# The last 64 channels' low-part product in two 64-row halves of the array, in the tail of a vision-tower kernel

## The chip, the cores and the metric

The kernel runs on one core of one Trainium2 chip. The time is the device time of one execution in microseconds, the median of three runs. A profile of one execution stands beside it: its span goes from the first to the last instruction, and its own device time is given with it.

## The reference

Two images of 32 channels and 128 x 128 pixels become 256 tokens each. A token mixer (patch embedding to 128 channels, two transformer layers) is followed by a head to 192 channels. The tail works at that width, and is the part that the change touches:

```
h   = _ln(x, lnf_g, lnf_b) @ head_w + head_b          # 256 tokens x 192 channels
# linear attention, 12 heads of 16, _phi(x) = elu(x) + 1
qkv = _layernorm(h) @ W_qkv                           # 192 -> 3 x 192
...                                                   # k^T v, q (k^T v) / z
h   = h + attention @ W_out + b_out
# feed-forward, weights multiplied by a mask that is mixed from alpha_e, alpha_r
h   = h + gelu(_layernorm(h) @ w_fc + b_fc) @ w_proj + b_proj     # 192 -> 768 -> 192
```

(The tail's lines are abridged here into one form; the products and their sizes are the reference's.)

## The kernel before

The program is written out by hand, one instruction list per engine, with counting semaphores between them. Nothing but the order of the lines sets the order of the work. The two images go through the same steps, and one image's products are placed where the other waits for VectorE (DVE) or ScalarE (ACT).

TensorE (PE) multiplies 32-bit numbers in two ways here. Plain products (`head`, `attend3`, `numerators3`, `proj3`, the transposes) take their operands as they are. Products that need accuracy at the fast rate are split: each operand is the sum of a high part and a low part, both of type fp32r, and the product is high x high + high x low + low x high. In the tail two products are split: `rows192` (query and key together 384 columns wide as `qk3_high`/`qk3_low`, the value 192 wide as `v3_rows`) and `fc3` (six chunks of 128 hidden units by 256 tokens).

The 192 channels don't fit the 128 rows of the array. Channels 0 to 127 are one contraction of 128 rows: three products, high x high, high x low, low x high. The last 64 channels are stacked: rows 0 to 63 of `yT3_rest` hold the input's high part, rows 64 to 127 its low part, and the host has put the weight's rows 128 to 191 in both halves. One product with the weight's high part (`aqkvw_parts[0][:, 1, :]`, `fcw_parts[0][:, 1, :]`) gives high x high + low x high. One more with the weight's low part gives high x low; for it the rows 64 to 127 of the weight's low part are set to zero, so half of the array multiplies zeros. That is five products for each output: L454, L455, L457, L458, L459 in `rows192`, L503 to L507 in `fc3`.

The input parts are made after a transpose (`turn3`, L339 and L340) into PSUM: DVE writes the high part (`high_part3`, L1046), ACT copies the last 64 channels' high part (`evict`, L1558), DVE writes their low part into rows 64 to 127 (`rest_low_part3`) and then the low part of the first 128 (`low_part3`, both L969). ACT turns the qk product into the elu feature (L1593, L1597), scales the value (L1601) and computes the gelu (L1607). `fc3`'s chunks lie two to a PSUM bank, and so do the value's two token tiles.

Two 64-row products side by side are in the kernel already, in `value_out` (L390): its odd and even products take rows 0 to 63 and 64 to 127, and write two banks.

Of the kernel before, what the change touches and what calls it, by code (L numbers as in the profile page):

```python
# [12 lines left out]
P = 128  # L13
# [11 lines left out]
E = 192  # L25
# [32 lines left out]
def build(nc, small, convb, norm_rows0, norm_rows1, ff_norm_rows0, ff_norm_rows1, embed0, patches1, qkv_w, rest_w, rows, mix, fc_w, proj_w,  # L58
          head_w, aqkv_w, aout_w, out):
    with ExitStack() as ctx:  # L60
# [64 lines left out]
        def bias_row(name, n=0, width=D):  # L125
# [17 lines left out]
        yT3_hi, yT3_lo, yT3_rest = (per_image(f"yT3_{part}", [P, TOKENS], F32R) for part in ("hi", "lo", "rest"))  # L143
# [59 lines left out]
        TURN4_BANK = [bank[3], bank[5]]  # L203
        TURN4_REST_BANK = [bank[4], bank[1]]
        V3_BANK = [bank[3], bank[0]]
# [6 lines left out]
        PROJ3_BANK = [(bank[0], bank[3]), (bank[4], bank[5])]  # L212
        FC3_BANK = [(bank[3], bank[2], bank[6]), (bank[5], bank[0], bank[0])]
# [42 lines left out]
            sem(n) for n in ("y_ready", "y_turned",))  # L256
        consts_set = sem("consts_set")
# [54 lines left out]
        def _(pe):  # L312
# [136 lines left out]
            def rows192(dst, i, t, at, stages):  # L449


                tile = slice(t * P, (t + 1) * P)
                if "high" in stages:
                    nc.tensor.matmul(dst, yT3_hi[i][:, tile], aqkvw_parts[0][:, 0, at], start=True, stop=False)  # L454
                    mm = nc.tensor.matmul(dst, yT3_hi[i][:, tile], aqkvw_parts[1][:, 0, at], start=False, stop=False)  # L455
                if "low" in stages:
                    nc.tensor.matmul(dst, yT3_lo[i][:, tile], aqkvw_parts[0][:, 0, at], start=False, stop=False)  # L457
                    nc.tensor.matmul(dst, yT3_rest[i][:, tile], aqkvw_parts[0][:, 1, at], start=False, stop=False)  # L458
                    mm = nc.tensor.matmul(dst, yT3_rest[i][:, tile], aqkvw_parts[1][:, 1, at], start=False, stop=True)  # L459
                return mm  # L460

            def qk3_high(i, t):
                return rows192(QK3_BANK[i][t][:, 0:2 * E], i, t, slice(0, 2 * E), ("high",))

            def qk3_low(i, t):
                return rows192(QK3_BANK[i][t][:, 0:2 * E], i, t, slice(0, 2 * E), ("low",))

            def v3_rows(i, t):
                return rows192(V3_BANK[i][:, t * E:(t + 1) * E], i, t, slice(2 * E, 3 * E), ("high", "low"))

# [15 lines left out]
            def numerators3(i):  # L486
                for t in range(TILES):
                    for c in range(ECH):
                        at = (t * ECH + c) * KVW
                        mm = nc.tensor.matmul(NUM3_BANK[i][:, at:at + KVW], qT3[i][:, c, t * P:(t + 1) * P],  # L490
                                              kv3[i][:, c, :], start=True, stop=True)
                return mm

            def attend3(i, t):
                for c in range(ECH):
                    mm = nc.tensor.matmul(ATT3_BANK[i][:, t * E:(t + 1) * E], attT3[i][:, c, t * P:(t + 1) * P],  # L496
                                          aoutw[:, c, :], start=(c == 0), stop=(c == ECH - 1))
                return mm

            def fc3(i, c):  # L500
                at = slice(c * P, (c + 1) * P)
                dst = FC3_BANK[i][c // 2][:, (c % 2) * TOKENS:(c % 2 + 1) * TOKENS]
                nc.tensor.matmul(dst, fcw_parts[0][:, 0, at], yT3_hi[i][:], start=True, stop=False)  # L503
                nc.tensor.matmul(dst, fcw_parts[1][:, 0, at], yT3_hi[i][:], start=False, stop=False)
                nc.tensor.matmul(dst, fcw_parts[0][:, 0, at], yT3_lo[i][:], start=False, stop=False)
                nc.tensor.matmul(dst, fcw_parts[0][:, 1, at], yT3_rest[i][:], start=False, stop=False)
                return nc.tensor.matmul(dst, fcw_parts[1][:, 1, at], yT3_rest[i][:], start=False, stop=True)  # L507
# [46 lines left out]
            pe.wait_ge(consts_set, 14)  # L554
# [275 lines left out]
            qk3_high(0, 0)  # L830
            qk3_high(0, 1)
# [8 lines left out]
            v3_rows(0, 0).then_inc(v3_done, 1)  # L840
            v3_rows(0, 1).then_inc(v3_done, 1)
# [21 lines left out]
            v3_rows(1, 0).then_inc(v3_done, 1)  # L863
            v3_rows(1, 1).then_inc(v3_done, 1)
# [14 lines left out]
            fc3(0, 2).then_inc(fc3_done, 1)  # L879
            pe.wait_ge(gelu3_ready, 1)  # L880
            proj3(0, 0, 0).then_inc(proj3_done, 1)
            pe.wait_ge(attention3_columns, 2)
            attend3(1, 0).then_inc(out3_done, 1)
            attend3(1, 1).then_inc(out3_done, 1)
            pe.wait_ge(gelu3_ready, 2)
            proj3(0, 0, 1).then_inc(proj3_done, 1)
            fc3(0, 3).then_inc(fc3_done, 1)
            proj3(0, 1, 0).then_inc(proj3_done, 1)
            proj3(0, 1, 1).then_inc(proj3_done, 1)
            pe.wait_ge(gelu3_ready, 3)  # L890
# [4 lines left out]
            fc3(0, 4).then_inc(fc3_done, 1)  # L895
            fc3(0, 5).then_inc(fc3_done, 1)
# [8 lines left out]
            proj3(0, 5, 1).then_inc(proj3_done, 1)  # L905
            pe.wait_ge(low4, 2)
            fc3(1, 0).then_inc(fc3_done, 1)
            fc3(1, 1).then_inc(fc3_done, 1)
            pe.wait_ge(out_ready, 1)
            fc3(1, 2).then_inc(fc3_done, 1)  # L910
            fc3(1, 3).then_inc(fc3_done, 1)
            pe.wait_ge(gelu3_ready, 7)
            proj3(1, 0, 0).then_inc(proj3_done, 1)
            pe.wait_ge(gelu3_ready, 8)
            proj3(1, 0, 1).then_inc(proj3_done, 1)
            proj3(1, 1, 0).then_inc(proj3_done, 1)
            proj3(1, 1, 1).then_inc(proj3_done, 1)
            pe.wait_ge(gelu3_ready, 9)
# [3 lines left out]
            fc3(1, 4).then_inc(fc3_done, 1)  # L922
            fc3(1, 5).then_inc(fc3_done, 1)
# [10 lines left out]
        def _(dve):  # L934
# [116 lines left out]
            def rest_low_part3(i, bankof):  # L1051
                return low_part(yT3_rest[i][EB:P, :], bankof[0:EB, 0:TOKENS], yT3_rest[i][0:EB, :])
# [56 lines left out]
            dve.wait_ge(consts_set, 14)  # L1109
# [336 lines left out]
            rest_low_part3(0, TURN3_REST_BANK[0])  # L1446
# [32 lines left out]
            dve.wait_ge(rest_high3, 2)  # L1479
            rest_low_part3(1, TURN3_REST_BANK[1])  # L1480
# [33 lines left out]
            rest_low_part3(0, TURN4_REST_BANK[0])  # L1514
# [25 lines left out]
            dve.wait_ge(rest_high4, 2)  # L1540
            rest_low_part3(1, TURN4_REST_BANK[1])
# [14 lines left out]
        def _(act):  # L1556
# [43 lines left out]
            def v3_to_sbuf(i, t):  # L1600
                return nc.scalar.activation(v3[i][:, t, :, 0:EC],  # L1601
                                            V3_BANK[i][:, t * E:(t + 1) * E].rearrange("p (n e) -> p n e", e=EC),
                                            ACT.Copy, scale=rstd[i][:, t:t + 1])

            def gelu3(i, c):
                src = FC3_BANK[i][c // 2][:, (c % 2) * TOKENS:(c % 2 + 1) * TOKENS]
                return nc.scalar.activation(hid3[i][:, c, :], src, ACT.Gelu_apprx_tanh, bias=fcb[:, c:c + 1])  # L1607
# [157 lines left out]
            evict(yT3_rest[0][0:EB, :], TURN3_REST_BANK[0][0:EB, 0:TOKENS]).then_inc(rest_high3, 1)  # L1765
            act.wait_ge(qk3_done, 1)
# [14 lines left out]
            evict(yT3_rest[1][0:EB, :], TURN3_REST_BANK[1][0:EB, 0:TOKENS]).then_inc(rest_high3, 1)  # L1781
            act.wait_ge(qk3_done, 3)
# [14 lines left out]
            evict(yT3_rest[0][0:EB, :], TURN4_REST_BANK[0][0:EB, 0:TOKENS]).then_inc(rest_high4, 1)  # L1797
            act.wait_ge(fc3_done, 2)
# [11 lines left out]
            evict(yT3_rest[1][0:EB, :], TURN4_REST_BANK[1][0:EB, 0:TOKENS]).then_inc(rest_high4, 1)  # L1810
            act.wait_ge(fc3_done, 8)
# [10 lines left out]
        def _(pool):  # L1822
# [41 lines left out]
            pool.wait_ge(consts_set, 14)  # L1864
# [3 lines left out]
            low_part(aqkvw_parts[1][0:EB, 1, :], aqkvw[0:EB, 1, :], aqkvw_parts[0][0:EB, 1, :])  # L1868
# [63 lines left out]
            low_part(fcw_parts[1][0:EB, 1, :], fcw[0:EB, 1, :], fcw_parts[0][0:EB, 1, :])  # L1932
# [81 lines left out]
```

## Time and profile before

| what | us |
|---|---|
| median of 3 runs | 129.16 (128.75 to 129.81) |
| profiled execution, device time | 129.22 |
| its span | 126.8 |
| PE busy | 117.3 (93%) |
| DVE busy | 77.0 (61%) |
| ACT busy | 62.9 (50%) |
| GpSimd (POOL) busy | 45.9 (36%) |

The device time is 2.4 us more than the span; that is the launch and the end, which the span leaves out. The tail begins near 87.5 us. Records of PE overlap: a matmul's record has its whole way through the array in it, so what one product costs a busy PE is the distance from its start to the next start, not its length.

### The profile page before, as it was taken

The page shows a single profiled execution, that of the slowest core. Times are in us where ns is not written, and L with a number is a line of the kernel's source. Part 1 is how long each engine was busy: PE and PEld are TensorE (multiplying, and loading weights), DVE is VectorE, ACT ScalarE, POOL GpSimd, SP SyncE. Part 2 cuts the span into 40 slices and gives each one's busy share as a digit, 9 for nine tenths or more (in the row PEclk, how much of TensorE's full clock was granted, in tenths as well). Part 3 has the DMA queues.
Part 4 walks back from the last instruction along what each step waited for, and adds up shares of the span by engine and source line. Part 5 has one row for each costly group of instructions (what it writes and reads, how often), then busy time and mean ns, then how long its engine had stood idle before and what let it go on. Part 6 is the DMA issues. An engine that isn't in the chain of part 4 may idle for free.

```text
span 126.8 us, 2258 instructions
## 1 busy us (share of the span) xinstructions
PE 117.3 (93%) x852; PEld 101.2 (80%) x852; DVE 77.0 (61%) x244; ACT 62.9 (50%) x151; POOL 45.9 (36%) x56
## 2 busy tenths in 40 slices
PE   6999979999999999999999899977989988999991
PEld 6989968985978778997856689966777877998990
DVE  5000264996787766679999897639498377155002
ACT  4000142844579478194774876534871735423520
POOL 0000024034599833204939858475214032031000
PEclk9999999999999999999999999999999999999999
DMA  4999799999600000000000000000000000000101
GB/s 106 353 418 433 228 435 393 386 421 414 185 0 0 0 3 5 0 0 0 0 0 5 0 0 0 3 5 0 0 0 0 0 0 5 0 0 0 62 0 62
DMA packets 4171, 12.43 MB, mean 98 GB/s; under 512 B 473, under 2 KB 2105, under 8 KB 3906
## 3 DMA queue, kind: packets, MB, share of 16 engines
q1 hardware_dynamic: 4162, 12.31, 26.0%
q8 instruction: 6, 0.10, 0.3%
q14 instruction: 3, 0.02, 0.1%
HBM read 11.91 MB, written 0.39 MB: 97 GB/s over the span
## 4 chain that ended last, share of the span: by engine, by line
PE 65%; DVE 12%; DMA 9%; ACT 4%; issue 3%; SPq 3%; POOL 2%; DVEq 0%; ACTq 0%; POOLq 0%
DMA norm_rows_sb<-in_norm_rows 9%; PE bank L405 6%; PE bank L510 6%; PE bank L424 5%; PE bank L381 4%; PE bank L325 4%; PE bank L398 3%; PE bank L376 3%; SPq L265 3%; PE bank L346 3%; PE bank L412 2%; PE bank L358 2%; PE bank L496 2%; PE bank L334 2%; PE bank L390 2%
## 5 line engine op out<-in xcount | busy, mean ns | idle before, releaser
L1824 POOL TENSOR_TENSOR rstd<-mv,minus_half 128x2 f32<-128x2 f32 x14 | 10.0, 716 | 47.8 <-DVE mv L942 47.8
L1842 POOL TENSOR_TENSOR qn<-q,rqsum 128x512 f32<-128x512 f32 x8 | 8.3, 1042 | 10.5 <-DVE rqsum L1012 10.5
L1607 ACT ACTIVATE patches_sb<-bank,fcb 128x256 f32<-128x256 f32 x12 | 5.1, 469 | 10.5 <-PE bank L507 10.5
L1565 ACT ACTIVATE kexp<-bank,nkmax 128x256 f32<-128x256 f32 x16 | 7.5, 472 | 5.7 <-DVE nkmax L992 5.7
L405 PEld LDWEIGHTS bank<-cw,qT 128*128 128x128 f32 x64 | 8.0, 191 | 2.4 <-issue 1.5
L405 PE MATMUL bank<-cw,qT 128*128 128x128 f32 x64 | 8.9, 280 | 0.7 <-DVE x L1027 0.4
L510 PE MATMUL bank<-projw,patches_sb 128*128 128x192 f32 x48 | 9.4, 331 | 0.0
L325 PE MATMUL bank<-embed_sb 128*128 128x128 f32 x64 | 8.7, 291 | 0.3 <-DMA embed_sb<-in_embed 0.3
L424 PE MATMUL bank<-restw,hid 128*128 128x128 f32 x64 | 8.8, 281 | 0.1
L325 PEld LDWEIGHTS bank<-embed_sb 128*128 128x128 f32 x64 | 8.0, 200 | 1.1 <-DMA embed_sb<-in_embed 1.1
L1558 ACT ACTIVATE x<-bank 128x128 f32<-128x128 f32 x4 | 1.1, 282 | 14.4 <-DVE stats L936 14.4
L1581 ACT ACTIVATE hid<-bank,small_sb 128x256 f32<-128x256 f32 x16 | 6.5, 472 | 3.6 <-PE bank L419 3.6
L424 PEld LDWEIGHTS bank<-restw,hid 128*128 128x128 f32 x64 | 7.8, 191 | 0.6 <-issue 0.3
L936 DVE BATCH_NORM_STATS2 stats<-bank 128x6 f32<-128x128 f32 x4 | 1.1, 274 | 11.7 <-PE bank L330 11.6
L510 PEld LDWEIGHTS bank<-projw,patches_sb 128*128 128x128 f32 x48 | 7.6, 189 | 0.5 <-ACT patches_sb L1607 0.4
L381 PE MATMUL bank<-ktok,y 128*128 128x512 f32 x16 | 8.0, 612 | 0.0
L325 PE MATMUL bank<-embed_sb,patches_sb 128*128 128x128 f32 x64 | 7.9, 277 | 0.0
L325 PEld LDWEIGHTS bank<-embed_sb,patches_sb 128*128 128x128 f32 x64 | 7.5, 192 | 0.2 <-DMA patches_sb<-in_patches 0.2
L992 DVE TENSOR_REDUCE nkmax<-bank 128x2 f32<-128x512 f32 x8 | 5.4, 688 | 3.0 <-PE bank L365 2.9
L1834 POOL TENSOR_TENSOR xb<-x,rows_sb 128x256 f32<-128x256 f32 x8 | 5.8, 730 | 3.6 <-DVE xn L978 2.4
L969 DVE TENSOR_TENSOR yT_lo<-bank,yT_hi 128x256 fp32r<-128x256 f32 x12 | 5.1, 422 | 2.9 <-ACT yT_hi L1558 2.8
L1577 ACT ACTIVATE cw<-bank,rksum 128x128 f32<-128x128 f32 x16 | 4.8, 364 | 3.8 <-PE bank L398 3.8
(165 smaller groups left out, 333.0 us busy)
## 6 DMA issues: line engine op xcount, KB each, us to landing
embed_sb<-in_embed SPq DMA_DIRECT2D x3, 768.0 KB, 7.7
patches_sb<-in_patches SPq DMA_DIRECT2D x2, 1024.0 KB, 12.5
restw<-in_rest_w SPq DMA_DIRECT2D x2, 768.0 KB, 15.6
qkvw<-in_qkv_w SPq DMA_DIRECT2D x3, 256.0 KB, 11.7
qkvw<-in_qkv_w SPq DMA_DIRECT2D x1, 768.0 KB, 15.7
fcw<-in_fc_w SPq DMA_DIRECT2D x1, 768.0 KB, 18.3
embed_sb<-in_embed SPq DMA_DIRECT2D x1, 576.0 KB, 4.4
aqkvw<-in_aqkv_w SPq DMA_DIRECT2D x1, 576.0 KB, 12.2
```

Source lines behind the costliest of these rows:

```text
L325: mm = nc.tensor.matmul(CONV_BANK[i][t][:, 0:D], left, embed_sb[:, c, 0:D], start=(c == 0), stop=False)
L381: return nc.tensor.matmul(YK_BANK[s][:], y[s % IMAGES][:, t, :], ktok[:, t, :], start=(t == 0), stop=(t == TILES - 1))
L405: mm = nc.tensor.matmul(ATT_BANK[s][t][:, 0:D], qT[:, t, c * P:(c + 1) * P], cw[:, c, :], start=(c == 0), stop=(c == PAIRS - 1))
L424: mm = nc.tensor.matmul(FF2_BANK[s][t][:, 0:D], hid[:, c, t * P:(t + 1) * P], ff2w(s // IMAGES, c), start=(c == 0), stop=(c == FC - 1))
L510: return nc.tensor.matmul(PROJ3_BANK[i][t][:, 0:E], hid3[i][:, c, t * P:(t + 1) * P], projw[:, c, :], start=(c == 0), stop=(c == HC - 1))
L969: return nc.vector.tensor_tensor(lo, exact, hi.bitcast(F32), ALU.subtract)
L992: return nc.vector.tensor_reduce(nkmax[i][:, 2 * b:2 * b + 2], K_BANK[s][b][:].rearrange("p (c t) -> p c t", c=2), AX_X, ALU.max, negate=True)
L1565: return nc.scalar.activation(kexp[:, c, :], K_BANK[s][c // 2][:, (c % 2) * TOKENS:(c % 2 + 1) * TOKENS], ACT.Exp, bias=nkmax[i][:, c:c + ...
L1581: return nc.scalar.activation(hid[:, c, :], FF1_BANK[s][c // 2][:, (c % 2) * TOKENS:(c % 2 + 1) * TOKENS], ACT.Gelu, bias=col("ff1_b", s / ...
L1824: return nc.gpsimd.tensor_tensor(rstd[i][:], mv[i][:, :, 1], minus_half[:], ALU.pow)
L1834: return nc.gpsimd.tensor_tensor(xb[i][:], x[i][:], row.unsqueeze(1).to_broadcast([P, TILES, D]), ALU.add)
L1842: return nc.gpsimd.tensor_tensor(qn[:, t, :].rearrange("p (h d) -> p h d", h=HEADS), q[:, t, :].rearrange("p (h d) -> p h d", h=HEADS), rq ...
```

## The change

The zero half of the array is given work. The weight's low part now holds its 64 rows twice (no zeros). Two outputs are worked on together: after the high products and the products with the weight's high part, the low-part product of the first output runs in rows 0 to 63 and that of the second in rows 64 to 127. The second needs the input's high part in rows 64 to 127 as well, so ACT makes a copy, `rest3_copy`, four times. Each of the two outputs needs its own PSUM bank; `FC3_BANK`, `V3_BANK`, `PROJ3_BANK` and the transposes' banks are dealt out anew. The products with `yT3_lo` come last. In the feed-forward PE starts on the high part (`high4`) instead of waiting for `low4`, the chunks come in pairs, and projections are moved behind them. DVE loses two memsets at the start; POOL subtracts all 128 rows where it did 64.

```diff
-        V3_BANK = [bank[3], bank[0]]
+        V3_BANK = [(bank[3], bank[0]), (bank[0], bank[5])]
-        PROJ3_BANK = [(bank[0], bank[3]), (bank[4], bank[5])]
-        FC3_BANK = [(bank[3], bank[2], bank[6]), (bank[5], bank[0], bank[0])]
+        PROJ3_BANK = [(bank[0], bank[4]), (bank[1], bank[7])]
+        FC3_BANK = [bank[3], bank[2], bank[6], bank[5], bank[3], bank[2]]
...
+            def rows192_rest(bank_of, i, at, n):
+                for t in range(TILES):
+                    nc.tensor.matmul(bank_of[t][:, 0:n], yT3_rest[i][:, t * P:(t + 1) * P], aqkvw_parts[0][:, 1, at],
+                                     start=False, stop=False)
+                for t in range(TILES):
+                    rows, left = slice(t * EB, (t + 1) * EB), (yT3_rest, rest3_copy)[t]
+                    mm = nc.tensor.matmul(bank_of[t][:, 0:n], left[i][rows, t * P:(t + 1) * P],
+                                          aqkvw_parts[1][rows, 1, at], start=False, stop=False)
+                return mm
...
+            def fc3_rest(i, pair):
+                for c in (2 * pair, 2 * pair + 1):
+                    nc.tensor.matmul(FC3_BANK[c][:, 0:TOKENS], fcw_parts[0][:, 1, c * P:(c + 1) * P], yT3_rest[i][:],
+                                     start=False, stop=False)
+                for odd in range(2):
+                    rows, c, right = slice(odd * EB, (odd + 1) * EB), 2 * pair + odd, (yT3_rest, rest3_copy)[odd]
+                    mm = nc.tensor.matmul(FC3_BANK[c][:, 0:TOKENS], fcw_parts[1][rows, 1, c * P:(c + 1) * P],
+                                          right[i][rows, :], start=False, stop=False)
+                return mm
...
+            pe.wait_ge(high4, 1)
+            fc3_high(0, 0)
+            pe.wait_ge(rest_low4, 1)
+            pe.wait_ge(rest_high4, 2)
+            fc3_rest(0, 0)
             pe.wait_ge(low4, 1)
-            fc3(0, 0).then_inc(fc3_done, 1)
-            fc3(0, 1).then_inc(fc3_done, 1)
+            fc3_low(0, 0).then_inc(fc3_done, 1)
+            fc3_low(0, 1).then_inc(fc3_done, 1)
...
-            nc.vector.memset(aqkvw_parts[1][EB:P, 1, :].bitcast(F32), 0.0).then_inc(consts_set, 1)
-            nc.vector.memset(fcw_parts[1][EB:P, 1, :].bitcast(F32), 0.0).then_inc(consts_set, 1)
...
             evict(yT3_rest[0][0:EB, :], TURN3_REST_BANK[0][0:EB, 0:TOKENS]).then_inc(rest_high3, 1)
+            act.wait_ge(rest_high3, 1)
+            evict(rest3_copy[0][EB:P, :], yT3_rest[0][0:EB, :].bitcast(F32)).then_inc(rest_high3, 1)
...
-            low_part(fcw_parts[1][0:EB, 1, :], fcw[0:EB, 1, :], fcw_parts[0][0:EB, 1, :])
+            low_part(fcw_parts[1][:, 1, :], fcw[:, 1, :], fcw_parts[0][:, 1, :])
```

The qk product of image 0 on PE (token tile 0 in bank 5, tile 1 in bank 1), from the first high product on; before:

```order
L454 MATMUL bank5<-aqkvw_hi,yT3_hi0 128x384 [waits high3]
L455 MATMUL bank5<-aqkvw_lo,yT3_hi0 128x384
L454 MATMUL bank1<-aqkvw_hi,yT3_hi0 128x384
L455 MATMUL bank1<-aqkvw_lo,yT3_hi0 128x384
L457 MATMUL bank5<-aqkvw_hi,yT3_lo0 128x384 [waits low3]
L458 MATMUL bank5<-aqkvw_hi,yT3_rest0 128x384
L459 MATMUL bank5<-aqkvw_lo,yT3_rest0 128x384
```

and with the change:

```order
L455 MATMUL bank5<-aqkvw_hi,yT3_hi0 128x384 [waits high3]
L455 MATMUL bank5<-aqkvw_lo,yT3_hi0 128x384
L455 MATMUL bank1<-aqkvw_hi,yT3_hi0 128x384
L455 MATMUL bank1<-aqkvw_lo,yT3_hi0 128x384
L463 MATMUL bank5<-aqkvw_hi,yT3_rest0 128x384 [waits rest_high3,rest_low3]
L463 MATMUL bank1<-aqkvw_hi,yT3_rest0 128x384
L467 MATMUL bank5<-aqkvw_lo,yT3_rest0 128x384
L467 MATMUL bank1<-aqkvw_lo,rest3_copy0 128x384
L472 MATMUL bank5<-aqkvw_hi,yT3_lo0 128x384 [waits low3]
```

Tile 0 used to be finished after seven products; it is now finished after nine, the two L467 being the 64-row pair. For image 1 it was finished after five (high, high, low, rest, rest), and is now finished after nine too.

The first two hidden chunks of the feed-forward of image 0 on PE; before:

```order
L503 MATMUL bank3<-yT3_hi0,fcw_hi 128x256 [waits low4]
L504 MATMUL bank3<-yT3_hi0,fcw_lo 128x256
L505 MATMUL bank3<-yT3_lo0,fcw_hi 128x256
L506 MATMUL bank3<-yT3_rest0,fcw_hi 128x256
L507 MATMUL bank3<-yT3_rest0,fcw_lo 128x256
L503 MATMUL bank3<-yT3_hi0,fcw_hi 128x256
```

and with the change:

```order
L524 MATMUL bank3<-yT3_hi0,fcw_hi 128x256 [waits high4]
L524 MATMUL bank3<-yT3_hi0,fcw_lo 128x256
L524 MATMUL bank2<-yT3_hi0,fcw_hi 128x256
L524 MATMUL bank2<-yT3_hi0,fcw_lo 128x256
L531 MATMUL bank3<-yT3_rest0,fcw_hi 128x256 [waits rest_high4,rest_low4]
L531 MATMUL bank2<-yT3_rest0,fcw_hi 128x256
L535 MATMUL bank3<-yT3_rest0,fcw_lo 128x256
L535 MATMUL bank2<-rest3_copy0,fcw_lo 128x256
L540 MATMUL bank3<-yT3_lo0,fcw_hi 128x256 [waits low4]
L540 MATMUL bank2<-yT3_lo0,fcw_hi 128x256
```

The number of products is the same, ten for two chunks; two of them (L535) are now 64 rows each, and stand between products of all 128 rows.

ACT at the start of the tail, with the change; the second row is new:

```order
L1613 ACTIVATE yT3_rest0<-bank7 64x256 [waits turned3]
L1613 ACTIVATE rest3_copy0<-yT3_rest0 64x256 [waits rest_high3]
L1648 ACT_TABLE_LOAD [waits deviation3_ready]
L1648 ACTIVATE embed_sb<-bank5,rstd0 128x384 [waits qk3_done]
```

The copy stands ahead of the load of the exp table and of the first elu instruction.

## Rows read from the trace of the kernel before

**Rows 1.** The page: busy times of the engines.

```profile
PE 117.3 (93%) x852; PEld 101.2 (80%) x852; DVE 77.0 (61%) x244; ACT 62.9 (50%) x151; POOL 45.9 (36%) x56
```

**Rows 2.** Busy time by stretch, the feed-forward: stretch, its length, each engine, granted clock (1.00 is full).

```profile
106.30:123.90 17.60, 17.57 (x124) 16.70 (x124) 4.98 (x17) 6.18 (x15) 1.71 (x2) 1.00 0.04 11
```

**Rows 3.** PE's timeline around `value_out`: start us, us, instruction, rows*columns of the array.

```profile
33.95 0.28 PE L358 MATMUL bank<-yT_hi,qkw_lo 128*128 128x256 f32 x1
34.06 0.28 PE L365 MATMUL bank<-yT_lo,qkw_hi 128*128 128x256 f32 x1
34.27 1.16 PE L390 MATMUL bank<-restw,qkvw 64*128 64x128 f32 x16
35.36 0.50 PE L346 MATMUL bank<-qkw_hi,yT_hi 128*128 128x512 f32 x1
35.70 0.39 PE L346 MATMUL bank<-qkw_lo,yT_hi 128*128 128x512 f32 x1
35.93 0.40 PE L352 MATMUL bank<-qkw_hi,yT_lo 128*128 128x512 f32 x1
```

**Rows 4.** Line 390 by itself: duration ns min/median/max, first and last start.

```profile
L390 PE MATMUL bank<-restw,qkvw x32: 271/272/374, 34.3 to 52.6; 64*128 64x128 f32 x32
```

**Rows 5.** PE's timeline, the attention of image 0, then of image 1.

```profile
88.69 0.44 PE L454 MATMUL bank<-aqkvw_hi,yT_hi 128*128 128x384 f32 x1 [0.52 <-DVE yT_hi L1046]
88.97 0.34 PE L455 MATMUL bank<-aqkvw_lo,yT_hi 128*128 128x384 f32 x1
...
89.32 0.33 PE L455 MATMUL bank<-aqkvw_lo,yT_hi 128*128 128x384 f32 x1
89.58 0.44 PE L457 MATMUL bank<-aqkvw_hi,yT_lo 128*128 128x384 f32 x1
...
90.04 0.34 PE L459 MATMUL bank<-aqkvw_lo,yT_rest 128*128 128x384 f32 x1
...
93.15 0.27 PE L459 MATMUL bank<-aqkvw_lo,yT_rest 128*128 128x192 f32 x1
...
94.24 0.94 PE L474 MATMUL bank<-v,embed_sb 128*96 128x102 f32 x8
...
96.62 0.42 PE L454 MATMUL bank<-aqkvw_hi,yT_hi 128*128 128x384 f32 x1
...
97.66 0.34 PE L459 MATMUL bank<-aqkvw_lo,yT_rest 128*128 128x384 f32 x1
```

**Rows 6.** The chain of waits: start us, us, what.

```profile
90.41 0.58 ACT embed_sb L1593
...
98.04 0.67 ACT embed_sb L1597
```

**Rows 7.** ACT's timeline: the last 64 channels' copy, the table, the value.

```profile
88.21 0.38 ACT L1558 ACTIVATE yT_rest<-bank 64x256 fp32r<-64x256 f32 x1 [1.74 <-PE bank L340]
88.61 1.28 ACT L1593 ACT_TABLE_LOAD   x1
...
93.46 0.73 ACT L1601 ACTIVATE v<-bank,rstd 128x192 f32<-128x192 f32 x2 [0.50 <-PE bank L459]
```

**Rows 8.** PE's timeline: the start of each image's feed-forward, and what is ahead of it.

```profile
104.72 1.08 PE L490 MATMUL bank<-kv,patches_sb 96*128 96x102 f32 x8
106.29 0.39 PE L503 MATMUL bank<-yT_hi,fcw_hi 128*128 128x256 f32 x1 [0.49 <-DVE yT_lo L969]
106.51 0.28 PE L504 MATMUL bank<-yT_hi,fcw_lo 128*128 128x256 f32 x1
...
114.85 1.53 PE L510 MATMUL bank<-projw,patches_sb 128*128 128x192 f32 x8
116.42 0.39 PE L503 MATMUL bank<-yT_hi,fcw_hi 128*128 128x256 f32 x1
```

**Rows 9.** DVE's timeline: the input parts of the feed-forward.

```profile
104.92 0.42 DVE L1046 CAST yT_hi<-bank 128x256 fp32r<-128x256 f32 x1 [0.32 <-PE bank L340]
...
105.81 0.42 DVE L969 TENSOR_TENSOR yT_lo<-bank,yT_hi 128x256 fp32r<-128x256 f32 x1
```

More of the change, by code:

```diff
@@ L142, in build @@
         yT_hi, yT_lo = (per_image(f"yT_{part}", [P, TOKENS], F32R) for part in ("hi", "lo"))
-        yT3_hi, yT3_lo, yT3_rest = (per_image(f"yT3_{part}", [P, TOKENS], F32R) for part in ("hi", "lo", "rest"))
+        yT3_hi, yT3_lo, yT3_rest, rest3_copy = (
+            per_image(name, [P, TOKENS], F32R) for name in ("yT3_hi", "yT3_lo", "yT3_rest", "rest3_copy"))
         nkmax = per_image("nkmax", [P, PAIRS])
@@ L447, in head @@
                                         start=True, stop=True)
[L449 to L459, printed above, removed]
-                return mm
@@ L462, in qk3_high, with rows192 @@
-            def qk3_high(i, t):
-                return rows192(QK3_BANK[i][t][:, 0:2 * E], i, t, slice(0, 2 * E), ("high",))
-            def qk3_low(i, t):
-                return rows192(QK3_BANK[i][t][:, 0:2 * E], i, t, slice(0, 2 * E), ("low",))
-            def v3_rows(i, t):
-                return rows192(V3_BANK[i][:, t * E:(t + 1) * E], i, t, slice(2 * E, 3 * E), ("high", "low"))
+            def rows192(bank_of, i, at, n):
+                for t in range(TILES):
+                    for part in range(2):
+                        mm = nc.tensor.matmul(bank_of[t][:, 0:n], yT3_hi[i][:, t * P:(t + 1) * P],
+                                              aqkvw_parts[part][:, 0, at], start=(part == 0), stop=False)
+                return mm
@@ new lines, in rows192_rest @@
+            def rows192_rest(bank_of, i, at, n):
+                for t in range(TILES):
+                    nc.tensor.matmul(bank_of[t][:, 0:n], yT3_rest[i][:, t * P:(t + 1) * P], aqkvw_parts[0][:, 1, at],
+                                     start=False, stop=False)
+                for t in range(TILES):
+                    rows, left = slice(t * EB, (t + 1) * EB), (yT3_rest, rest3_copy)[t]
+                    mm = nc.tensor.matmul(bank_of[t][:, 0:n], left[i][rows, t * P:(t + 1) * P],
+                                          aqkvw_parts[1][rows, 1, at], start=False, stop=False)
+                return mm
@@ new lines, in rows192_low, with qk3_high, qk3_rest @@
+            def rows192_low(bank_of, i, t, at, n):
+                return nc.tensor.matmul(bank_of[t][:, 0:n], yT3_lo[i][:, t * P:(t + 1) * P], aqkvw_parts[0][:, 0, at],
+                                        start=False, stop=True)
+            def qk3_high(i):
+                return rows192(QK3_BANK[i], i, slice(0, 2 * E), 2 * E)
+            def qk3_rest(i):
+                return rows192_rest(QK3_BANK[i], i, slice(0, 2 * E), 2 * E)
+            def qk3_low(i, t):
+                return rows192_low(QK3_BANK[i], i, t, slice(0, 2 * E), 2 * E)
@@ L471, in context3, with v3_high_and_rest, v3_low @@
+            def v3_high_and_rest(i):
+                at = slice(2 * E, 3 * E)
+                rows192(V3_BANK[i], i, at, E)
+                return rows192_rest(V3_BANK[i], i, at, E)
+            def v3_low(i, t):
+                return rows192_low(V3_BANK[i], i, t, slice(2 * E, 3 * E), E)
             def context3(i):
@@ L498, in attend3, with fc3_high, fc3_low @@
                 return mm
[L500 to L507, printed above, removed]
+            def fc3_high(i, pair):
+                for c in (2 * pair, 2 * pair + 1):
+                    for part in range(2):
+                        mm = nc.tensor.matmul(FC3_BANK[c][:, 0:TOKENS], fcw_parts[part][:, 0, c * P:(c + 1) * P],
+                                              yT3_hi[i][:], start=(part == 0), stop=False)
+                return mm
+            def fc3_rest(i, pair):
+                for c in (2 * pair, 2 * pair + 1):
+                    nc.tensor.matmul(FC3_BANK[c][:, 0:TOKENS], fcw_parts[0][:, 1, c * P:(c + 1) * P], yT3_rest[i][:],
[4 more added lines that the diff above has]
+                                          right[i][rows, :], start=False, stop=False)
+                return mm
+            def fc3_low(i, c):
+                return nc.tensor.matmul(FC3_BANK[c][:, 0:TOKENS], fcw_parts[0][:, 0, c * P:(c + 1) * P], yT3_lo[i][:],
+                                        start=False, stop=True)
             def proj3(i, c, t):
@@ L1781, in _ @@
             evict(yT3_rest[1][0:EB, :], TURN3_REST_BANK[1][0:EB, 0:TOKENS]).then_inc(rest_high3, 1)
+            act.wait_ge(rest_high3, 3)
+            evict(rest3_copy[1][EB:P, :], yT3_rest[1][0:EB, :].bitcast(F32)).then_inc(rest_high3, 1)
             act.wait_ge(qk3_done, 3)
@@ L1797, in _ @@
             evict(yT3_rest[0][0:EB, :], TURN4_REST_BANK[0][0:EB, 0:TOKENS]).then_inc(rest_high4, 1)
+            act.wait_ge(rest_high4, 1)
+            evict(rest3_copy[0][EB:P, :], yT3_rest[0][0:EB, :].bitcast(F32)).then_inc(rest_high4, 1)
             act.wait_ge(fc3_done, 2)
@@ L1810, in _ @@
             evict(yT3_rest[1][0:EB, :], TURN4_REST_BANK[1][0:EB, 0:TOKENS]).then_inc(rest_high4, 1)
+            act.wait_ge(rest_high4, 3)
+            evict(rest3_copy[1][EB:P, :], yT3_rest[1][0:EB, :].bitcast(F32)).then_inc(rest_high4, 1)
             act.wait_ge(fc3_done, 8)
```

94 lines of the change are left out of this document (56 added, 38 removed).

## The prediction

> **What bounds the kernel now.** I read the page first. PE is busy for 93% of the span [rows 1], so the question is what an edit costs PE. In the tail the busy times by stretch come next: from 106.3 us to 123.9 us, the two feed-forwards, PE is busy 17.57 of 17.60 us at full granted clock [rows 2]. There each 0.1 us more or less on PE moves the end by as much. Ahead of that, from 88 to 106 us, PE and ACT take turns. The chain of waits goes through ACT's first elu instruction of each image, L1593 at 90.41 and L1597 at 98.04 [rows 6], and both start when L459 ends, the product that finishes token tile 0: 90.04 + 0.34 = 90.38, and 97.66 + 0.34 = 98.00 [rows 5]. So two clocks count: when tile 0 of the query and key product is finished, and how long PE is occupied afterwards.
>
> The slot of one product is the distance between starts. At 256 columns it is 0.11 us (33.95 to 34.06) [rows 3]. At 384 columns I take 0.17 us, half of 89.32 less 88.97 [rows 5]. A first product after a stand costs more: 88.69 to 88.97 is 0.28 for 384 columns, 0.11 above the slot, because its weight load is not hidden.
>
> **What a lone 64-row pair costs.** The only 64-row pairs in the trace are those of `value_out` [rows 3, 4]. Their 16 records (each fp32 product is recorded twice) begin at 34.27, and the last begins at 34.27 + 1.16 - 0.27 = 35.16. The longest record is 374 ns, the median 272: the first ones carry an exposed weight load of 0.10. The rest is (0.89 - 0.10) / 7 = 0.11 us for each two records, so inside such a run two records do fit in one slot. The edges are another matter. Entry: 34.06 to 34.27 is 0.21 where the slot is 0.11, 0.10 lost. Exit: 35.16 to 35.36 is 0.20, 0.09 lost. The next 128-row product then takes 35.36 to 35.70 = 0.34 where the following takes 35.70 to 35.93 = 0.23: 0.11 more for its exposed load. Entry 0.10, load 0.10, exit 0.09, load 0.11: 0.40 us of edges. `value_out` has eight products to spread them over; the change makes a run of one pair, ten times, each between 128-row products. What it saves is one slot: 0.11 us at 256 or 192 columns, 0.17 at 384. So a pair costs PE 0.40 - 0.11 = **+0.29 us**, or +0.23 at 384 columns. No row shows fp32r operands in half the array, hence the bounds: with no edges -0.11 (-0.17), with edges and the two one behind the other +0.40. I take +0.29, since the run of line 390 is entered from fp32r products and left to them, as here.
>
> The Trainium skill ("TensorE: Matmul & The Clock Gate", Measured speedup vs the span model) has packed tiles take the time of one matmul and some 4 ns for each further tile; by that alone every pair would save its slot, and the sum below would be about -1.3 instead of +2.3. The trace agrees inside the run, not at its edges. The same skill ("TensorEngine Tiling (Array Packing)", Key Properties) says that a change of tiling mode drains the engine, and gives no time for it; the entry and exit gaps are what this trace shows of it.
>
> **Part by part.**
>
> - *Tile 0 of query and key, image 0.* High products start at 88.69, 88.97, 89.15, 89.32 as now [rows 5]. Then the two with the weight's high part, 89.49 and 89.66; the pair at 89.66 + 0.17 + 0.10 = 89.93; load 0.10, its columns 0.17, exit 0.09: the low product at 90.29, and with the exposed load it takes 0.44 as L457 does now: done at 90.73, against 90.38. **+0.35** on the chain. The present wait for the low part (89.32 to 89.58) goes, and is in this.
> - *The value, image 0.* ACT starts it only when both tiles are finished: 93.15 + 0.27 = 93.42, start 93.46 [rows 5, 7], and PE's next product waits for ACT: 93.46 + 0.73 = 94.19, start 94.24 [rows 5, 7]. One pair makes the value later by 0.29, less what PE waits now: **+0.25**.
> - *Tile 0, image 1.* It was finished after five products and now after nine. From 96.62 [rows 5]: 96.90, 97.07, 97.24, 97.41, 97.58, pair 97.85, low 98.21, done 98.65 against 98.00: **+0.65**, through ACT's L1597, the attention's columns, W_out and the norm up to the feed-forward.
> - *The value, image 1.* The same delay, but the next transpose waits for the norm as well. Between 0 and 0.26 I take **+0.15**.
> - *Start of the feed-forward, image 0.* PE now waits for `low4`, written until 105.81 + 0.42 = 106.23 [rows 9], start 106.29. The high part is there at 104.92 + 0.42 = 105.34 [rows 9], so PE is free to start behind L490, whose last record starts at 104.72 + 1.08 - 0.28 = 105.52: at 105.63 [rows 8]. **-0.66**. The rest part (done when L969 starts on the low part, 105.81) and the low part (106.23) are needed only after four and seven more products, 105.63 + 0.11 + 4 x 0.11 = 106.18 and later, so they are in time.
> - *Start of the feed-forward, image 1.* The last projection record starts at 114.85 + 1.53 - 0.33 = 116.05, one slot of its kind, half its 0.33, gives 116.21 against 116.42 [rows 8]: **-0.20**.
> - *Six pairs of chunks.* 6 x 0.29 = **+1.74**, all in the stretch where PE has no idle time [rows 2].
> - *The copies.* ACT's `rest3_copy` reads 64x256, as the copy before it does in 0.38 [rows 7]. Image 0: 88.59 to about 88.98, the table load of 1.28 then ends at 90.26, and the first elu can't start before 90.73: covered, by 0.47. PE needs the copy at 89.93. In the feed-forward the copy ends at about 105.7 and is needed after 106.18. Cost 0; if ACT were later than that, PE would stand, and the pair's start would show it.
> - *Projections moved behind the chunk pairs, new banks.* Same products; more of PE's work lies between a chunk and its projection, so gelu is later needed, not earlier. 0. DVE's two memsets lie before the first patch arrives, and POOL's subtraction of 128 rows instead of 64 handles the same columns: 0.
>
> Sum: 0.35 + 0.25 + 0.65 + 0.15 - 0.66 - 0.20 + 1.74 = **+2.28 us**. The span becomes 126.8 + 2.3 = 129.1, the device time 129.22 + 2.28 = **131.5 us**. The profiled execution lies 0.06 above the median 129.16, which changes nothing. That is 1.8% slower.
>
> **Rivals.**
>
> - *The pairs pack without edges* (faster). Then tile 0 is finished at 90.34 and 98.26, -0.04 and +0.26; the values cost nothing; the six pairs save 0.66, and the starts 0.86: -0.04 + 0.26 - 0.66 - 0.86 = -1.3, **127.9 us**. For it speaks the 0.11 us per two records inside the run; against it the entry and exit gaps. It decides once the edges cost less than the slot saved, 0.11 us. 7%.
> - *Cheap edges.* Only one exposed load is left at each end and the drains overlap, edges of 0.20: +0.09 for a pair, 0.54 for six, some 0.5 in the attention, -0.86: +0.2, **129.4 us**. 8%.
> - *The attention absorbs its delays.* ACT and DVE wait much there, and if the four terms 0.35, 0.25, 0.65, 0.15 vanish, 2.28 - 1.40 = +0.9, **130.1 us**. Against it: both elu starts follow L459 by 0.03 [rows 5, 6]. 9%.
> - *The halves don't overlap* with fp32r operands: another 0.11 for eight pairs and 0.17 for two, +1.1, **132.6 us**. 8%.
>
> My forecast has 68%. The range 129.9 to 132.6 takes in the last two rivals and an edge cost of 0.33 to 0.50; it leaves out the first two, 15%. One per cent, 1.3 us, is about what a measurement of this kernel can tell from no change. Slower by over that, above 130.45: 0.68, most of it, with the 0.08 and small parts of the others: 0.78. Within: 0.16. Faster, below 127.87: half of the first rival and a little for what I don't see, 0.06.
>
> **What the profile of the changed kernel would show.** A gap of 0.2 us ahead of each first half product and of 0.3 us from it to the next 128-row product; 17.6 + 1.7 + what starts earlier in the feed-forward's busy time; L1648 at about 90.8, against 90.41; PE's first feed-forward product right behind the numerators, waiting for nothing. The forecast fails if the distance from the first half product to the next full one is near 0.11, or if ACT's elu starts are unmoved.

## The result, and the profile after

The changed kernel takes 131.26 us (median, 130.63 to 132.09) against 129.13 us for the kernel before (128.75 to 129.81): ratio 1.0176, 95% interval 1.0134 to 1.0218, that is 1.7 to 2.8 us. It is slower by 2.1 us; 131.5 was forecast.

The profiled execution took 131.63 us with a span of 129.4, so 2.6 more than the span before. Not all of that is the change's. The first high product of image 0's attention, where the first changed product on PE stands, starts at 88.69 before [rows 5] and at 89.45 after. The shift comes from the loads ahead of it. Sixteen of the patch products start at 22.60 us before, without a wait; in PE's timeline after they wait for DMA and start 0.67 later:

```profile
23.27 2.05 PE L327 MATMUL bank<-embed_sb,patches_sb 128*128 128x128 f32 x16 [0.74 <-DMA patches_sb<-in_patches]
```

This wait comes and goes between executions. e4 below, whose memsets are those of the kernel before, has it too, 0.91 us. Over the twelve profiled executions of this study the first high product lies anywhere from 87.88 to 89.58, with the same instructions on PE ahead of it in all. So I compare profiles from that product to the end of the span, and call the stretch the tail. It was 126.8 - 88.69 = 38.11 us, and is 129.4 - 89.45 = 39.95: **+1.84 us** for the change there. The medians differ by 2.13. The interval of the medians has both numbers in it, so whether the remaining 0.29 is spread, or a cost of the change ahead of the tail (two memsets less, POOL's 128 rows), stays open.

PE's timeline after, image 0's attention first, then image 1's, then the start of the feed-forward (start us, us, instruction, rows*columns of the array used):

```profile
89.45 0.44 PE L455 MATMUL bank<-aqkvw_hi,yT_hi 128*128 128x384 f32 x1 [0.52 <-DVE yT_hi L1103]
...
90.25 0.51 PE L463 MATMUL bank<-aqkvw_hi,yT_rest 128*128 128x384 f32 x2
90.69 0.44 PE L467 MATMUL bank<-aqkvw_lo,yT_rest 64*128 64x384 f32 x1
90.69 0.44 PE L467 MATMUL bank<-aqkvw_lo,rest_copy 64*128 64x384 f32 x1
91.06 0.45 PE L472 MATMUL bank<-aqkvw_hi,yT_lo 128*128 128x384 f32 x1
...
95.62 0.94 PE L495 MATMUL bank<-v,embed_sb 128*96 128x102 f32 x8
...
98.00 0.42 PE L455 MATMUL bank<-aqkvw_hi,yT_hi 128*128 128x384 f32 x1
...
99.59 0.44 PE L472 MATMUL bank<-aqkvw_hi,yT_lo 128*128 128x384 f32 x1
...
106.92 1.14 PE L511 MATMUL bank<-kv,patches_sb 96*128 96x102 f32 x8
107.84 0.36 PE L524 MATMUL bank<-yT_hi,fcw_hi 128*128 128x256 f32 x1
...
108.39 0.40 PE L531 MATMUL bank<-yT_rest,fcw_hi 128*128 128x256 f32 x2
108.72 0.38 PE L535 MATMUL bank<-yT_rest,fcw_lo 64*128 64x256 f32 x1
108.72 0.38 PE L535 MATMUL bank<-rest_copy,fcw_lo 64*128 64x256 f32 x1
109.03 0.50 PE L540 MATMUL bank<-yT_lo,fcw_hi 128*128 128x256 f32 x2
109.42 0.64 PE L504 MATMUL bank<-small_sb,embed_sb 128*96 128x128 f32 x4
...
117.15 1.47 PE L544 MATMUL bank<-projw,patches_sb 128*128 128x192 f32 x8
118.32 0.42 PE L524 MATMUL bank<-yT_hi,fcw_hi 128*128 128x256 f32 x1
```

The two halves of a pair start at the same hundredth, at 90.69 and at 108.72: they run side by side (e5 below takes this away, and it costs). The second L531 starts at 108.39 + 0.40 - 0.28 = 108.51; the pair 0.21 later, the next full product 0.31 after the pair, and the second L540 at 109.03 + 0.50 - 0.28 = 109.25, 0.22 on. That is 0.74 us where four slots are 0.45: 0.29 for the pair.

ACT's timeline after, the new copy and what is behind it:

```profile
89.38 0.41 ACT L1613 ACTIVATE rest_copy<-yT_rest 64x256 fp32r<-64x256 f32 x1
89.81 1.28 ACT L1648 ACT_TABLE_LOAD   x1
91.55 0.58 ACT L1648 ACTIVATE embed_sb<-bank,rstd 128x384 f32<-128x384 f32 x1 [0.45 <-PE bank L472]
...
94.83 0.73 ACT L1656 ACTIVATE v<-bank,rstd 128x192 f32<-128x192 f32 x2 [0.74 <-PE bank L472]
```

ACT waits 0.45 us for PE after the copy and the table load, so this copy costs nothing. After each of the other three, and the table load that follows one of them, ACT waits for PE as well, between 0.50 and 2.21 us. The elu starts 91.55 - 89.45 = 2.10 us into the tail; the forecast's 90.8 is 2.11.

Busy time by stretch after, from the first feed-forward product on, which answers to [rows 2]: PE has no idle time here either, and 1.13 us more work, where 1.74 was forecast for the pairs.

```profile
107.80:126.50 18.70, 18.70 (x127) 17.04 (x125) 5.51 (x19) 7.68 (x16) 1.70 (x2) 1.00 0.03 11
```

### The profile page after: what moved, and what is told of

Read it like the earlier page. It is cut to its first block, busy times and chain, and to the rows that moved or that the text cites. A ratio compares the mean times of both kernels' runs of the same rounds, so it can differ in the third digit from the quotient of the medians.

```text
span 129.4 us, 2264 instructions
## 1 busy us (share of the span) xinstructions
PE 118.2 (91%) x852; PEld 100.9 (78%) x852; DVE 75.9 (59%) x242; ACT 64.7 (50%) x155; POOL 45.9 (35%) x56
## 4 chain that ended last, share of the span: by engine, by line
PE 65%; DMA 12%; DVE 8%; SPq 5%; ACT 4%; issue 2%; POOL 1%; ACTq 0%
DMA patches_sb<-in_patches 12%; PE bank L407 6%; PE bank L544 6%; SPq L267 5%; PE bank L426 5%; PE bank L383 4%; PE bank L400 3%; PE bank L327 3%; PE bank L378 3%; PE bank L414 2%; PE bank L517 2%; PE bank L524 2%; PE bank L540 2%; PE bank L455 2%; PE bank L336 2%
## 5 line engine op out<-in xcount | busy, mean ns | idle before, releaser
L544 PE MATMUL bank<-projw,patches_sb 128*128 128x192 f32 x48 | 8.6, 326 | 0.0
```

## The experiments

The tails of all profiled executions, next to the medians and the ratios to the kernel before on the same chip (its median there was 129.15 for e1 to e4, 129.04 for e5 to e8, 129.47 for e9 and e10, so read the ratios, not the times, across these groups). Spans are printed to a tenth, so a tail is good to 0.05 us:

| kernel | time us | ratio (95%) | tail us |
|---|---|---|---|
| before | 129.13 | | 38.11 |
| changed | 131.26 | 1.0176 (1.0134 to 1.0218) | 39.95 |
| e1 all full height | 128.89 | 0.9972 (0.9938 to 1.0006) | 37.79 |
| e2 feed-forward pairs only | 130.07 | 1.0063 (1.0039 to 1.0087) | 39.17 |
| e3 attention pairs only | 129.41 | 1.0018 (0.9987 to 1.0049) | 38.42 |
| e4 tile 0 first | 128.05 | 0.9915 (0.9885 to 0.9946) | 36.92 |
| e5 same half | 132.79 | 1.0284 (1.0243 to 1.0324) | 41.02 |
| e6 lone halves | 134.06 | 1.0393 (1.0356 to 1.0431) | 42.98 |
| e7 joined pairs | 131.31 | 1.0176 (1.0141 to 1.0212) | 40.09 |
| e8 filled wait | 127.79 | 0.9911 (0.9883 to 0.9938) | 36.71 |
| e9 late last pair | 129.51 | 0.9993 (0.9954 to 1.0031) | 37.94 |
| e10 start on high | 128.61 | 0.9943 (0.9912 to 0.9975) | 37.64 |

The theory throughout: a 64-row pair between full-height products costs PE more in its edges than the slot it saves, and the rest of the change is worth something.

### e1: everything else of the change, without the pairs

```diff
-                for odd in range(2):
-                    rows, c, right = slice(odd * EB, (odd + 1) * EB), 2 * pair + odd, (yT3_rest, rest3_copy)[odd]
-                    mm = nc.tensor.matmul(FC3_BANK[c][:, 0:TOKENS], fcw_parts[1][rows, 1, c * P:(c + 1) * P],
-                                          right[i][rows, :], start=False, stop=False)
+                for c in (2 * pair, 2 * pair + 1):
+                    mm = nc.tensor.matmul(FC3_BANK[c][:, 0:TOKENS], fcw_parts[1][:, 1, c * P:(c + 1) * P],
+                                          yT3_rest[i][:], start=False, stop=False)
```

and the same in the attention; memsets back, copies out.

> The changed kernel's order, banks and waits, but the low-part products of the last 64 channels use all 128 rows again (zeros in the lower half, no copies, the two memsets back). Edge theory (a lone 64-row pair costs PE 0.29 us more than two full products, 0.23 at 384 columns): the six feed-forward pairs give back 1.74, the two qk pairs 0.46, the two value pairs 0.25 and 0.15, together 2.6: time near 128.7, and 37.35 us from the first high product of the attention to the end (39.95 in the changed kernel). Rival 'the attention absorbs its pairs': only 1.74 comes back, 129.5. Rival 'the loss is in the new order, the banks or the copies': the time stays over 130.5.

Measured: 128.89 us, tail 37.79. The pairs are the loss: without them the changed kernel is no slower than the one before, and its banks and its order are still in place. But 2.16 us came back, not 2.6. PE's timeline of e1 shows the place, between the first two chunks and the transpose of image 1's heads:

```profile
107.29 0.39 PE L538 MATMUL bank<-yT_lo,fcw_hi 128*128 128x256 f32 x2
108.09 0.64 PE L503 MATMUL bank<-small_sb,embed_sb 128*96 128x128 f32 x4 [0.42 <-DVE embed_sb L1139]
```

The last chunk product starts at 107.29 + 0.39 - 0.28 = 107.40 and the transpose 0.69 us later, where 0.17 us lie between the same two in the changed kernel (109.25 to 109.42). PE is early and waits for DVE's attention output. So what the early start wins runs partly into this wait, and in the changed kernel the first pair's edges lie in it.

### e2 and e3: the pairs in one stage only

Full height as in e1 for the attention alone (e2), or for the feed-forward alone (e3).

> The changed kernel with full-height products in the attention, 64-row pairs in the feed-forward alone. Edge theory: 6 x 0.29 = 1.74 above the all-full kernel, time near 130.4, tail near 39.1. Rival 'the pairs pack and something else is slow': at or below the all-full kernel.

> The changed kernel with 64-row pairs in the attention alone. Edge theory with ACT's waits: 0.23 + 0.25 + 0.23 + 0.15 = 0.86 above the all-full kernel, time near 129.5, tail near 38.2. Rival 'the attention absorbs them': equal to the all-full kernel.

Measured against e1: the feed-forward's pairs cost 1.38 us of tail and 1.2 us of time, the attention's 0.63 and 0.5. Both are costs, each about a fifth or a quarter smaller than expected. The wait of e1 accounts for it, as it takes up part of either. From start to start it is 0.69 in e1, 0.41 in e2 and 0.44 in e3, so 0.28 of e2's 6 x 0.29 = 1.74 is covered, and 0.25 of the attention's delay. That leaves 1.46 for e2 and 0.6 for e3. The rival that the attention absorbs its pairs is out.

### e4: tile 0 first

```diff
-            qk3_high(1)
+            qk3_high(1, 0)
             pe.wait_ge(rest_low3, 2)
...
-            qk3_rest(1)
+            qk3_rest(1, 0)
             pe.wait_ge(low3, 2)
             qk3_low(1, 0).then_inc(qk3_done, 1)
+            qk3_high(1, 1)
```

> All full-height, the feed-forward in the changed order, and in the attention token tile 0 finished first: after seven products in image 0 and after five in image 1. Theory (the first elu of each image follows tile 0): against the all-full kernel tile 0 is ready 1 x 0.17 and 4 x 0.17 earlier, 0.86 less: time near 127.8, tail near 36.5, faster than the kernel before by 1%. Rival 'the elu is not what the chain waits for': equal to the all-full kernel.

Measured: 0.87 us less tail than e1 where 0.86 was expected, 128.05 us. The rival, that the elu is not what the chain waits for, is out. The order by tile matters by itself: image 1's elu follows the ninth product in e1 and the fifth here. Against the kernel before this is a gain, ratio 0.9915 with an interval that ends at 0.9946.

### e5: both halves in the same rows

```diff
-                    rows, c, right = slice(odd * EB, (odd + 1) * EB), 2 * pair + odd, (yT3_rest, rest3_copy)[odd]
+                    rows, c, right = slice(0, EB), 2 * pair + odd, yT3_rest
```

and likewise in the attention.

> The changed kernel with both low-part products of every pair in rows 0 to 63 of the array (the copies stay but are read by nothing). Theory that the two halves of the changed kernel really run side by side: the second product now starts a slot after the first instead of 0.003 us after it, 0.11 at 256 and 192 columns and 0.17 at 384; the entry and exit gaps stay as they are. Six times 0.11 and about 0.45 in the attention: near 1.1 over the changed kernel, 132.4. Rival 'a pair costs two slots anyway': no change, 131.3. Rival 'the edges belong to the two halves' change-over, not to the 64-row mode': faster than the changed kernel.

Measured: 132.79 us, 1.5 over the changed kernel's median; the tail is 1.07 us longer. In PE's timeline of e5 the two records of the second line below span 0.49 where one takes 0.38:

```profile
109.08 0.40 PE L531 MATMUL bank<-yT_rest,fcw_hi 128*128 128x256 f32 x2
109.40 0.49 PE L535 MATMUL bank<-yT_rest,fcw_lo 64*128 64x256 f32 x2
109.83 0.50 PE L540 MATMUL bank<-yT_lo,fcw_hi 128*128 128x256 f32 x2
```

From the second L531 (109.20) to the first L535 it is still 0.20 us, and from the second L535 (109.40 + 0.49 - 0.27 = 109.62) to L540 0.21. The concurrency of the changed kernel is real and worth its slot; the edges stay without it. They belong to the change between 128 and 64 rows, not to two halves at once.

### e6: the halves apart

```diff
-                for c in (2 * pair, 2 * pair + 1):
-                    nc.tensor.matmul(FC3_BANK[c][:, 0:TOKENS], fcw_parts[0][:, 1, c * P:(c + 1) * P], yT3_rest[i][:],
-                                     start=False, stop=False)
                 for odd in range(2):
                     ...
+                    mm = nc.tensor.matmul(FC3_BANK[c][:, 0:TOKENS], fcw_parts[0][:, 1, c * P:(c + 1) * P],
+                                          yT3_rest[i][:], start=False, stop=False)
```

> The changed kernel; in the feed-forward the two halves of a pair no longer stand together: each half product stands between products of 128 rows (half, full, half, full). Edge theory: a second set of edges of 0.40 and a slot of 0.11 for each pair, 0.51 x 6 = 3.1 more: 134.3, and a distance of 0.2 ahead of and 0.3 behind each half. Rival 'the cost is a fixed one for each pair or comes from the copies or banks': no change, 131.3.

Measured: tail +3.03 us over the changed kernel, 134.06 us. PE's timeline of e6:

```profile
107.26 0.28 PE L524 MATMUL bank<-yT_hi,fcw_lo 128*128 128x256 f32 x1
107.47 0.38 PE L532 MATMUL bank<-yT_rest,fcw_lo 64*128 64x256 f32 x1
107.79 0.38 PE L534 MATMUL bank<-yT_rest,fcw_hi 128*128 128x256 f32 x1
108.10 0.38 PE L532 MATMUL bank<-rest_copy,fcw_lo 64*128 64x256 f32 x1
108.41 0.38 PE L534 MATMUL bank<-yT_rest,fcw_hi 128*128 128x256 f32 x1
```

Each change of height, either way, now takes 0.31 or 0.32 us from start to start where a slot is 0.11; only the first entry takes 0.21. I read the difference as the weight load of the full product ahead, which is hidden there and exposed in the others. Doubling the number of mode changes has added what one set of edges and a slot were priced at, six times.

### e7: two pairs in one run

```diff
             fc3_high(1, 0)
+            fc3_high(1, 1)
...
-            fc3_rest(1, 0)
+            fc3_rest_two(1)
```

`fc3_rest_two` issues four full products and then the four halves.

> The changed kernel; in image 1 the first two pairs of chunks are worked on together, so that their four half products stand in one run. Edge theory: one set of edges less, 0.40: 130.9, and the stretch from the first high product of image 1's feed-forward to the first projection behind it takes 2.6 us instead of 3.0. Rival 'each pair costs 0.29 wherever it stands': 3.0 stays.

PE's timeline of e7:

```profile
117.96 0.42 PE L524 MATMUL bank<-yT_hi,fcw_hi 128*128 128x256 f32 x1
...
119.56 0.38 PE L546 MATMUL bank<-yT_rest,fcw_lo 64*128 64x256 f32 x1
119.57 0.38 PE L546 MATMUL bank<-rest_copy,fcw_lo 64*128 64x256 f32 x1
119.79 0.27 PE L546 MATMUL bank<-yT_rest,fcw_lo 64*128 64x256 f32 x1
119.79 0.27 PE L546 MATMUL bank<-rest_copy,fcw_lo 64*128 64x256 f32 x1
119.99 0.72 PE L551 MATMUL bank<-yT_lo,fcw_hi 128*128 128x256 f32 x4
121.06 1.57 PE L555 MATMUL bank<-projw,patches_sb 128*128 128x192 f32 x8 [0.34 <-ACT patches_sb L1671]
```

The last low product starts at 119.99 + 0.72 - 0.27 = 120.44, a slot later it is 120.55: 2.59 us for the two pairs, 3.00 in the changed kernel. The edge theory's 0.40 is there. The time is not: all four chunks are now finished at the end of the run, gelu starts later, and PE stands before the first projection, 0.62 us from start to start where 0.11 would do. Up to that projection, which is what the expectation named, the stretch takes 3.10. The expectation was right on PE's work and wrong on the stretch and the time, 131.31 us and a tail of 40.09, neither of which fell.

### e8: the wait filled

```diff
+            fc3_one(0, 3).then_inc(fc3_done, 1)
             pe.wait_ge(attention3_ready, 4)
             turn_heads(AT3_BANK[1], att3[1]).then_inc(attention3_turned, 1)
-            fc3_high(0, 1)
-            fc3_rest(0, 1)
-            fc3_low(0, 2).then_inc(fc3_done, 1)
-            fc3_low(0, 3).then_inc(fc3_done, 1)
+            fc3_one(0, 2).then_inc(fc3_done, 1)
```

> The tile0_first kernel with the fourth chunk of image 0's feed-forward (five full-height products, 0.57 us) moved ahead of the transpose of the second image's heads. There PE waits 0.70 us less a slot for DVE's attention output in the tile0_first and all-full kernels. Theory 'that wait is what the early start runs into': 0.57 less, near 127.5, tail 36.35. Rival 'the transpose's chain (attention, output, norm of image 1) is what bounds the second feed-forward': what is won is given back at the second image's transposes, 128.0.

Measured: 127.79 us and a tail of 36.71, 0.21 less than e4's, not 0.57. The wait before the transpose is gone; part of it has moved on to the output product, which now comes up against ACT's copy of the turned heads. From PE's timeline of e8:

```profile
107.96 0.28 PE L553 MATMUL bank<-yT_lo,fcw_hi 128*128 128x256 f32 x1
108.33 1.57 PE L522 MATMUL bank<-aoutw,qkvw 96*128 96x192 f32 x8
```

0.37 us from start to start where the slot is 0.11, and the run of eight itself takes 1.57 where e4's takes 1.46. Together that is 0.37, the missing 0.36. ACT's copy ends at 107.68 + 0.59 = 108.27. It is the fastest kernel here, ratio 0.9911, but the times of e4 and e8 don't tell them apart.

### e9: the projections back

The e1 kernel with its last two chunks behind the third chunk's projections:

```diff
+            proj3(1, 2, 0).then_inc(proj3_done, 1)
+            proj3(1, 2, 1).then_inc(proj3_done, 1)
             fc3_high(1, 2)
             ...
-            proj3(1, 2, 0).then_inc(proj3_done, 1)
-            proj3(1, 2, 1).then_inc(proj3_done, 1)
```

> The all-full kernel, with the last two chunks of each image's feed-forward moved one step back, behind the third chunk's projections, as in the kernel before. Theory that the changed kernel won 0.4 us because its projections stand further behind their chunks and no longer wait for gelu: short waits come back between the projections behind those chunks, two of about 0.1 us in each image (0.24 and 0.27 from start to start where the slot is 0.16), so the stretch from the first feed-forward product to the end is 0.2 to 0.4 longer than the all-full kernel's. Rival 'those waits were the earlier kernel's PSUM sharing, not the order': no such gaps, no change.

A run of n projection records should take (n - 1) x 0.163 + 0.33 us. The last run of the kernel is, in e1 and in e9, one row each of PE's timeline:

```profile
121.24 2.76 PE L542 MATMUL bank<-projw,patches_sb 128*128 128x192 f32 x16
```

```profile
121.57 2.29 PE L542 MATMUL bank<-projw,patches_sb 128*128 128x192 f32 x12
```

Sixteen fit (2.78); twelve should take 2.12 and take 2.29. The waits are back in image 1, 0.17 us, and the tail is 0.15 longer than e1's, just under the 0.2 to 0.4 expected. In image 0 they are not: its runs after the last pair fit. So the order is one cause of these waits, shown for one image. For image 0 the rival of the banks stands untested: e10, which has the earlier order and all the earlier banks but the transposes', has its waits in both images.

### e10: the early start alone

The kernel before, with the first chunk of each image on the high part, then the rest, then the low part:

```diff
+            pe.wait_ge(high4, 1)
+            fc3_first(0, "high")
+            pe.wait_ge(rest_low4, 1)
+            fc3_first(0, "rest")
             pe.wait_ge(low4, 1)
-            fc3(0, 0).then_inc(fc3_done, 1)
+            fc3_first(0, "low").then_inc(fc3_done, 1)
```

> The kernel before, with one edit: the first chunk of each image's feed-forward starts on the high part, then takes the rest, and the low part last (the transposes' banks as in the changed kernel, since the early start needs them). All else stays, projections too. PE begins 0.66 earlier, can do four products, and waits for the low part at 106.23: 0.45 and for image 1 0.2 less: 128.5. Behind it, PE then stands before the transpose of image 1's heads for what is earlier than DVE's output, as in the all-full kernel: if that wait takes it all in image 0, only 0.2 stays: 128.9.

Measured: 128.61 us, ratio 0.9943, tail 0.47 less than before. The start gained 0.7 us (105.44 - 88.56 = 16.88 into the tail, before 17.60), and PE then takes 0.39 from start to start ahead of the heads' transpose, where 0.12 would do: a wait as foreseen, but not of all that was won. The time lies between the two that were named.

## Why the prediction was right, step by step

- *The pair costs 0.29.* Right: 0.74 us against four slots of 0.11. The bound without edges, and the rival built on it, is out by e1 (the pairs cost 2.16 us of tail). e5 and e6 price edges and slot apart, and both agree. The rival that the halves don't overlap is out by the start times, and e5 shows what it would have cost: 1.07 us of tail (its own terms, 8 x 0.11 + 2 x 0.17, add up to 1.22, though the forecast writes 1.1). The rival of cheap edges had 0.20 for them; they take 0.40. The Trainium skill ("TensorEngine Tiling (Array Packing)", Key Properties) says that changing the tiling mode drains the engine; what e5 and e6 show of it is 0.21 us from start to start ahead of a half and 0.20 or more behind it where the slot is 0.11. The Trainium skill's span model ("TensorE: Matmul & The Clock Gate", Measured speedup vs the span model) holds within a pair, whose halves start at the same hundredth, and leaves the edges out.
- *Tile 0, image 0*, +0.35: done 2.06 us into the tail (91.06 + 0.45 = 91.51), 1.69 before, +0.37.
- *The value, image 0*, +0.25: the next product at 6.17 into the tail (95.62), 5.55 before, +0.62, of which 0.37 is tile 0's: +0.25.
- *Tile 0, image 1*, +0.65: 99.59 + 0.44 = 100.03, 10.58 into the tail, 9.31 before. +1.27, less the 0.62: +0.65.
- *The value, image 1, and the early start*, +0.15 - 0.66: the feed-forward starts at 18.39, 17.60 before: +0.79. The numerators ahead of it tell the two apart: L511 starts at 17.47 (106.92), L490 at 16.03 before, +1.44, which is 0.17 over the 1.27; then 0.79 - 1.44 = -0.65. The sum of the terms up to there was 0.35 + 0.25 + 0.65 + 0.15 - 0.66 = +0.74.
- *Six pairs and image 1's start*, +1.74 - 0.20: the rest of the tail grew by 1.84 - 0.79 = 1.05, not 1.54. **This is the step that was mis-sized**, not in the pairs but in the item beside them, "Projections moved behind the chunk pairs, new banks ... 0". Before, three runs of projections are longer than their slots: ten records take 1.97 (1.80 by the slot), twelve take 2.29 (2.12), and the eight of [rows 8] take 1.53 (1.47). Two of them, from PE's timeline of the kernel before:

```profile
111.14 1.97 PE L510 MATMUL bank<-projw,patches_sb 128*128 128x192 f32 x10
...
121.92 2.29 PE L510 MATMUL bank<-projw,patches_sb 128*128 128x192 f32 x12
```

  Together that is 0.17 + 0.17 + 0.06 = 0.40 us of short waits between projections. In the changed kernel every run of eight takes 1.46 or 1.47 and that of sixteen 2.76. I wrote that gelu would be needed later and put the gain at nothing, as if PE never waited for it. The busy time by stretch, 17.57 of 17.60, seemed to say so: but records of 0.33 us overlap, and a stand of 0.1 us between them doesn't show as idle. The weight loads do show it. From the timeline of PE's weight loads (PEld) before, within that last run:

```profile
122.65 1.27 PEld L510 LDWEIGHTS bank<-projw,patches_sb 128*128 128x128 f32 x8 [0.21 <-ACT patches_sb L1607]
```

  L1607 is gelu. The page puts 0.4 us of idle of L510's weight loads down to it; after, the same loads have 0.0.

Two smaller misses nearly cancel. Image 1's start gained 0.30, not 0.20: the last projection record starts at 117.15 + 1.47 - 0.33 = 118.29 and the feed-forward 0.03 later (0.37 before), of which a longer first load takes back 0.03. And the heads' transpose cost 0.10 that I had not priced: from the product ahead of it to the one behind it are 0.57 us (109.25 to 109.82, where the next L524 starts), 0.47 before. The pieces are then 1.74 - 0.40 - 0.30 + 0.10 = 1.14 us, and 1.05 was measured; each is good to a few hundredths.

With -0.40 in the sum it is 1.88, and the tail grew by 1.84. That the time came out at +2.13, nearer 2.28 than the tail is, is luck: it is within the spread of the runs, and the traces bear out the pair's cost and the attention's terms, not the sum. The chain was also right that PE is the bound, but one piece was missed: PE's early start meets DVE's attention output, so one of the six pairs lies in a wait that the change itself opened. Against the kernel before it makes no difference; against e1 it is why undoing the pairs gives 2.16 and not 2.6.

## What to carry to other kernels

Half-height products can pay in long runs only: price the entry, the exit and the two exposed weight loads from the trace, here 0.40 us for a run, and set them against a slot saved for each pair, here 0.11, so that at 256 columns I estimate that a run needs four pairs to win anything (two are the most that was tried here); but a run that long finishes its outputs late, and what reads them may then be waited for. When an edit bundles a layout with an order, run the order without the layout: here the layout cost 2.2 us of tail, its order without it was no slower than the kernel before, and with tile 0 first (e4) it was almost 1% faster. And look for short waits in the length of a run of equal records and in the idle time of the weight loads, not in PE's busy share.

## What the runs showed of the hardware that I had not expected

- In the joined run the second pair starts 0.22 us after the first and the exit comes 0.20 after that, while a lone pair is left after 0.31: the exposed load is paid once for each run.
- A lone half costs as much as a lone pair: both are 0.21 from the product ahead and 0.31 to the product behind, at full granted clock.
- The start of the tail moved by 1.7 us between profiled executions whose instructions up to there are the same on PE. A difference of spans between two single profiles says little below that.
